# Newton stage of a two-layer transformer block: the third softmax kernel formed transposed, remainders in halves, a new order

## The reference, cut to what matters

```python
kernel1 = softmax(einsum('bhnd,bhmd->bhnm', Q, K_l))    # 256 x 64 per head
kernel2 = softmax(einsum('bhmd,bhkd->bhmk', Q_l, K_l))  # 64 x 64
kernel3 = softmax(einsum('bhmd,bhnd->bhmn', Q_l, K))    # 64 x 256
V0 = kernel2.T / max(sum(kernel2, axis=-2))
for _ in range(6):                                      # Newton iterations
    KV = K @ V
    V = 0.25 * V @ (13 I - KV @ (15 I - KV @ (7 I - KV)))
SV = (kernel1 @ V) @ (kernel3 @ values)
out = SV @ w_proj
```

## Time and profile before

| what | us |
|---|---|
| median of 3 runs (2047.25 to 2049.43) | 2047.33 |
| profiled execution, its own time | 2049.97 |
| its span, first to last instruction | 2048.2 |
| TensorE busy in the span | 1849.3 |
| VectorE busy | 1646.0 |
| ScalarE busy | 1097.7 |
| GpSimd busy | 932.4 |
| mean granted TensorE clock, share of full | 0.976 |

### The profile page before, as it was taken

The page is one execution under the profiler, slowest core; times in us unless marked ns, Lnnn a source line. Parts: engine busy times, 40 slices in busy tenths (PEclk is TensorE's granted clock), DMA queues, the critical chain, the costliest instruction groups (busy, mean ns, idle before and its releaser), DMA issues.

```text
span 2048.2 us, 66118 instructions
## 1 busy us (share of the span) xinstructions
PE 1849.3 (90%) x27529; PEld 1414.5 (69%) x27529; DVE 1646.0 (80%) x3968; ACT 1097.7 (54%) x2880; POOL 932.4 (46%) x913
## 2 busy tenths in 40 slices
PE   3999899998999688868999999999999999967887
PEld 2888566665788556656777777777777777754666
DVE  6666799999566699966888888888888888857997
ACT  1444233332344466645666666666666666636664
POOL 2000688886000277733444444444444444426886
PEclk9999999999899899988999999999999999998999
DMA  4000000000000000000000000000000000000001
GB/s 118 1 1 1 1 1 2 2 2 2 1 1 1 1 1 1 1 1 3 3 3 3 3 4 3 3 3 3 3 3 4 3 3 3 3 2 1 21 22 42
DMA packets 14601, 14.44 MB, mean 7 GB/s; under 512 B 1440, under 2 KB 12128, under 8 KB 14304
## 3 DMA queue, kind: packets, MB, share of 16 engines
q1 hardware_dynamic: 11104, 8.83, 1.5%
q10 hardware_dynamic: 3200, 1.37, 0.3%
HBM read 6.01 MB, written 4.19 MB: 5 GB/s over the span
## 4 chain that ended last, share of the span: by engine, by line
PE 62%; DVE 27%; issue 6%; ACT 4%; POOL 1%; DVEq 0%; DMA 0%; POOLq 0%; SPq 0%
PE acc L473 6%; PE acc L450 6%; PE acc L1666 6%; DVE arena L576 5%; PE acc L1656 5%; PE acc L1678 4%; DVE acc L894 2%; DVE arena L571 2%; DVE arena L907 2%; DVE arena L884 2%; PE acc L757 2%; PE acc L1708 2%; PE acc L464 2%; PE acc L1606 2%; PE acc L1589 2%
## 5 line engine op out<-in xcount | busy, mean ns | idle before, releaser
L1506 POOL TENSOR_TENSOR arena<-arena 128x288 f32<-128x288 f32 (+1 forms) x384 | 293.1, 770 | 456.6 <-ACT arena L1413 397.8
L931 POOL TENSOR_TENSOR arena<-arena 128x960 f32<-128x960 f32 (+2 forms) x74 | 177.7, 2401 | 299.5 <-DVE arena L900 204.6
L1413 ACT ACTIVATE arena<-acc 64x288 f32<-64x288 f32 x384 | 155.6, 405 | 141.0 <-PE acc L1684 133.7
L1232 DVE SCALAR_TENSOR_TENSOR arena<-acc,arena 128x288 f32<-128x288 f32 (+1 forms) x384 | 157.1, 409 | 68.6 <-PE acc L1678 38.9
L679 POOL TENSOR_TENSOR arena<-arena,quadcol 128x512 f32<-128x512 f32 x64 | 79.3, 1258 | 247.4 <-DVE arena L546 247.4
L425 ACT ACTIVATE arena<-acc,wib 128x256 f32<-128x256 f32 x256 | 100.5, 475 | 149.9 <-PE acc L464 149.9
L1017 PE MATMUL acc<-wguT,arena 128*128 128x352 f32 x256 | 105.2, 493 | 48.1 <-DVE arena L884 47.2
L1678 PE MATMUL acc<-arena 64*64 64x72 f32 (+1 forms) x3072 | 135.1, 224 | 11.7 <-DVE arena L1232 11.6
L1666 PE MATMUL acc<-arena 64*64 64x72 f32 (+1 forms) x3072 | 133.0, 223 | 13.5 <-DVE arena L1223 12.8
L1666 PEld LDWEIGHTS acc<-arena 64*64 64x64 f32 x3072 | 110.8, 133 | 46.5 <-issue 44.1
L1223 DVE SCALAR_TENSOR_TENSOR arena<-arena 128x256 f32<-128x256 f32 x192 | 107.7, 561 | 43.6 <-ACT arena L1413 41.0
(11 more groups left out here) (238 smaller groups left out, 4890.9 us busy)
## 6 DMA issues: line engine op xcount, KB each, us to landing
out_dram<-X SPq DMA_DIRECT2D x3, 1024.0 KB, 5.2
out_dram<-X SPq DMA_DIRECT2D x1, 512.0 KB, 3.2
wi<-in_wiT_dram ACTq DMA_DIRECT2D x1, 256.0 KB, 5.4
wout<-in_woT_dram ACTq DMA_DIRECT2D x1, 256.0 KB, 7.4
out_dram<-X SPq DMA_DIRECT2D x1, 256.0 KB, 2.3
out_dram<-X SPq DMA_DIRECT2D x2, 128.0 KB, 1.8
wqkv<-in_w_qkv_dram ACTq DMA_DIRECT2D x1, 192.0 KB, 8.3
arena<-in_w_down_dram SPq DMA_DIRECT2D x1, 176.0 KB, 3.0
```

The costliest lines, as they stand in the source:

```text
L931: pool.tensor_tensor(b3(y[k][:, part(u)]), b3(z[k][:, part(u)]), each(small[u % kept][:, 1, blocks(u)]), ALU.mult).then_inc(y_ready, 1)
L1232: dve.scalar_tensor_tensor(pm[s][:, group[g], cols], pn[s][:, group[g], cols], part, tm[s][:, group[g], cols], ALU.mult, ALU.add).then_inc ...
L1413: ins = act.mul(sq[s][rows, group[g], :], pn[s][other, group[g], 0:MW], part)
L1506: pool.tensor_tensor(tm[s][:, group[g], cols], pm[s][:, group[g], cols], sq[s][:, group[g], cols], ALU.subtract).then_inc(tm_ready, 1)
```

## The change

The third kernel is formed transposed at once. `scores3` and `max3` stay for the maxima (two reductions of two banks each in place of four), which are laid in rows of a mask, transposed (`turn_m3`) and added to spare rows of the queries (`lower3`); `keys` makes copies of the keys in which the other pair's rows hold ones. `turned3` then forms the lowered, transposed scores in one product, `exp3` exponentiates them in two instructions, and `start_w` gets the row sums from columns of ones in `vtok`. The 16 transposes and `copy3` go. The first kernel does the same with `expand_rows`, `masked_queries` and `lower1`, and the products with `pick` go. The second group's square and remainder are made in halves: ScalarE and VectorE each take 64 partitions of the product from PSUM and then change over. The queues are reordered. The second kernel's softmax works as before.

```diff
-            e3 = [cut(NP, SEQ) for _ in R]
+            kx = [cut(2, SEQ) for _ in R]
+            qm = [cut(2, SEQ) for _ in R]
+            kst = [cut(NQ, LM) for _ in R]
+            mov3 = [cut(2, P) for _ in R]
+            mov1 = [cut(2, SEQ) for _ in R]
-                def max3(n, s, q):
-                    dve.wait_ge(s3_done, n * NQ + q + 1)
-                    dve.tensor_reduce(sm[s][:, NMAX3, 2 * q:2 * q + 2], A[q].rearrange("p (t n) -> p t n", t=2), AX,
+                def max3(n, s, k):
+                    dve.wait_ge(s3_done, n * NQ + 2 * k + 2)
+                    dve.tensor_reduce(m3n[s].rearrange("p o (q t c) -> p (o q) t c", t=2, c=16)[:, 2 * k:2 * k + 2, :, 0],
+                                      psum[:, 2 * k:2 * k + 2, :].rearrange("p q (t n) -> p q t n", t=2), AX,
                                       ALU.max, negate=True).then_inc(max3_ready, 1)
+                def lower3(n, s):
+                    dve.wait_ge(m3T_done, n + 1)
+                    for t in range(2):
+                        ins = dve.scalar_tensor_tensor(mov3[s][:, t, :], mxp[0], pairmask[:, 1 - t:2 - t],
+                                                       qlx[s][:, 2 * t:2 * t + 2, :].rearrange("p h m -> p (h m)"),
+                                                       ALU.mult, ALU.add)
+                    ins.then_inc(mov3_ready, 1)
...
+                    for h, (rows, cols) in enumerate(halves):
+                        ins = dve.tensor_tensor(pairs(pm[s])[rows, :, :, LM:LM + HD],
+                                                kvp[s][rows, :, :, h * HD:(h + 1) * HD],
...
+                def remainder_half(n, s, it, h):
+                    rows, other = halves[h][0], halves[1 - h][0]
+                    iterate(dve, n, it, 1)
+                    dve.wait_ge(sq_done, step(n, it, 1))
+                    if h == 0:
+                        dve.wait_ge(sq_ready, turn(n, it, 1))
+                    dve.scalar_tensor_tensor(rm[s][rows, group[1], :], pm[s][rows, group[1], 0:LM], 7.0 * size[it],
+                                             pn[s][other, group[1], 0:LM], ALU.mult, ALU.subtract).then_inc(rm_ready, 1)
...
+                def lower1(n, s, t):
+                    dve.wait_ge(mxT_done, n + 1)
+                    dve.wait_ge(qm_ready, n + 1)
+                    dve.scalar_tensor_tensor(mov1[s][:, t, :], A[0][:, 0:SEQ], pairmask[:, 1 - t:2 - t], qm[s][:, t, :],
+                                             ALU.mult, ALU.add).then_inc(mov1_ready, 1)
...
+                def keys(n, s):
+                    act.wait_ge(qk_ready, n + 1)
+                    for t in range(2):
+                        ins = act.activation(kx[s][:, t, :], qkT[buf(n)][:, 1, :], ACT.Identity,
+                                             bias=rowhot[:, 2 - 2 * t:3 - 2 * t], scale=pairmask[:, t:t + 1])
+                    ins.then_inc(kx_ready, 1)
+                def masked_queries(n, s):
+                    act.wait_ge(qk_ready, n + 1)
+                    for t in range(2):
+                        ins = act.activation(qm[s][:, t, :], qkT[buf(n)][:, 0, :], ACT.Copy, scale=pairmask[:, t:t + 1])
+                    ins.then_inc(qm_ready, 1)
+                def exp3(n, s, k):
+                    act.wait_ge(s3T_done, n + 1)
+                    act.activation(flat(eT[s][:, 4 * k:4 * k + 4, :]),
+                                   psum[:, 2 * k:2 * k + 2, :].rearrange("p q n -> p (q n)"), ACT.Exp)\
+                       .then_inc(e3_ready, 1)
-                def copy3(n, s, q):
...
+                def square_half(n, s, it, h):
+                    rows, other = halves[h][0], halves[1 - h][0]
+                    act.wait_ge(sq_done, step(n, it, 1))
+                    if h == 1:
+                        act.wait_ge(rm_ready, turn(n, it, 1))
+                    act.mul(sq[s][rows, group[1], :], pn[s][other, group[1], 0:MW], 15.0 / (13.0 * size[it]))\
+                       .then_inc(sq_ready, 1)
...
+                    pool.tensor_tensor(kst[s], klx[buf(n)], rowhot[:, :].unsqueeze(2).broadcast_to([P, NQ, LM]), ALU.add)\
                         .then_inc(lk_ready, 1)
...
-                def turn3(n, s, q):
+                def turn_m3(n, s):
+                    pe.wait_ge(max3_ready, 2 * n + 2)
+                    pe.transpose(mxp[0], m3n[s][:, 0, :], ident[:, :]).then_inc(m3T_done, 1)
+                def turned3(n, s):
+                    pe.wait_ge(mov3_ready, n + 1)
+                    pe.wait_ge(kx_ready, n + 1)
                     for t in range(2):
                         for j in range(TPB):
+                            for q in range(NQ):
+                                mm = pe.matmul(A[q][:, t * SEQ + j * P:t * SEQ + (j + 1) * P],
+                                               kx[s][quad(q), t, j * P:(j + 1) * P], mov3[s][quad(q), t, :],
+                                               start=True, stop=True, skip_group_check=True)
+                    mm.then_inc(s3T_done, 1)
...
+                    for t in range(2):
+                        for j in range(TPB):
+                            for q in range(NQ):
+                                mm = pe.matmul(kvT[s][quad(q), t * P:(t + 1) * P], vtok[s][:, j, 2 * q + t, :],
+                                               eT[s][:, 2 * q + t, j * P:(j + 1) * P], start=(j == 0),
```

More of the change, by code:

```diff
@@ L1439, in a @@
                     if run:
-                        square(n, s, 0, 1)
+                        square_half(n, s, 0, 0)
                     if head:
@@ L1523, in g @@
                         remainder(n, s, 0, 0)
+                    if head:
+                        expand_rows(n + 1, o)
+                    if run:
                         remainder(n, s, 0, 1)
-                        remainder(n, s, 1, 0)
                     if head:
```

335 lines of the change are left out of this document (161 added, 174 removed), and 2 rows, old and new, of the table names.

## The result

The changed kernel takes 2080.51 us (median of four runs, 2078.34 to 2086.21) beside 2048.38 for the kernel before on the same chip: 1.0149 times as long, 95% interval 1.0132 to 1.0167, or 32 us. Forecast were 2041, in a range of 2000 to 2063.

A forecast was written before the change was run, and what follows sets the result against it. TensorE was taken to set the pace, VectorE to pass it after the change. 31 periods x (27.9 - 28.07) = -5.3, ramp +1.3, last block -2.4: -6.4 from 2049.97 gives 2043.6, set to 2041 for the median; range 2000 to 2063.

The forecast's parts named there:

- Putting it in order: Walk of the new order through one steady Newton block: VectorE's stretch plus the seam, 27.7 to 28.1 us, taken as 27.9.
- seam: Between blocks: about 4.0 us in which VectorE has only 2.4 us to do, so it idles 1.2 to 1.6.
- VectorE's stretch: From max2 to newton(4, 1) in a block: VectorE has work without a gap for 24.1 us.
- rival 3: VectorE's halves lose overlap on both sides: 0.7 us more per block, block 28.6, time 2063; chance 0.24.
- The latency that the halves save: Each Newton iteration's square and remainder: 0.85 us instead of 1.25, hidden in steady blocks, 2.4 gained in the last.
- The changeover, "nothing": ScalarE and VectorE swapping halves in each iteration: ScalarE's first half is done before VectorE's second, so no cost.
- TensorE's work: TensorE's busy time per block: 3.26 us removed and 1.31 added, so from 27.39 to 25.44.
- TensorE keeps the pace: First rival: VectorE's halves overlap like full-width work, TensorE sets the block at 26.9 us, time 2010; chance 0.26.
- Ends: Outside the steady blocks: kernel start costs nothing, the stage's ramp +1.3 us once, the last block -2.4.
- ScalarE's busy time: Per block: at least 6 us removed, new exponentials and copies added, so it falls to 16 or 16.5.
- 0.42 per half: Each VectorE half remainder, 256 elements per partition from PSUM: 0.417 us, 0.43 with the gap.
- VectorE's busy time: Per block, counted from start to start: 6.3 us removed, 9.8 added, from 22.9 to 26.4 to 26.5.

The follow-up runs named there:

- e1: Changed kernel with the second group's remainder whole again, from the copy in SBUF, ScalarE squaring both halves without waiting: 2059.18 us.
- e15: Changed kernel without the changeover, VectorE's two halves side by side where the whole remainder stands: 2140.26 us.
- e3: Kernel before with only the halves and the changeover between ScalarE and VectorE put in: 2142.98 us.
- e7: Kernel before with the halves but no changeover, ScalarE squaring both halves before VectorE takes its two: 2071.8 us.
- e17: Changed kernel with whole remainders, plus sixteen unread transposes per block given to TensorE: 2087.91 us.
- e19: Changed kernel as it is, plus sixteen unread transposes per block given to TensorE: 2098.22 us.
- e10: Changed kernel with the halves but no changeover, VectorE's first half one place earlier than the whole remainder stood: 2197.79 us.
- e2: Changed kernel with whole remainders, each issued twice, the first time into a spare tile: 2213.23 us.

## Why the prediction was wrong

The step that failed is **"Putting it in order", with the terms that it takes: a block of 27.9**. Its shape was right (VectorE without a gap from `max2` to `newton(4, 1)`, then a seam); the size of VectorE's stretch was not, nor was the way it took each iteration's halves to go.

- *VectorE's stretch: 24.1 us forecast.* In the timeline `max2` starts at 1400.79 and `newton(4, 1)` at 1425.40, and 0.37 later the next could start: 25.0. Of the 0.9 too little, 0.8 is the overlap lost in front of seven halves: each starts 0.03 after the end of a full-width instruction and not 0.08 before it (as at 1407.91). That was rival 3, which I had given 0.24. `lower3` takes 0.52 from start to start in place of 0.4, `lower1` 0.79 in place of 0.66, and the overlap kept at 1403.88 gives 0.1 back. The seam came out at the forecast's upper end: VectorE waits 0.49 + 0.42 + 0.72 = 1.6 there. Without these waits its queue fills 28.94 - 1.6 = 27.3 us, forecast 26.5, by rival 3 27.2. I had the rule and one side of it in a row, and counted only the side that the row showed. The sum closes, but it is a reading of the timeline: no run gives back the lost overlap alone, and work cut from VectorE returned 0.22 of itself.
- *"The latency that the halves save": 0.85 in place of 1.25 per iteration.* The way from ScalarE's first half to the last one's end takes 1.7 us per iteration in the changed kernel and 1.65 with whole remainders (e1): nothing is saved. VectorE's halves stand behind other work and come late.
- *The changeover, "nothing".* ScalarE waits 1.7 us per block for it. In the changed kernel it still saves 60 us against halves without it (e15); in the order before, it cost 71 (e3 against e7). My walk looked only at VectorE's waits for ScalarE, which are indeed absent, and not at the other direction.
- *TensorE's work: 25.44 forecast, 26.8 measured.* One of the four groups of transposes took a step of 0.44 in the blocks before and not 0.59. `turned3` fills 1.10 (from 1410.13, the end of the product before, to 1411.23) and not 0.90; `start_w` fills 1.01, as forecast. Work added or taken away moves the busy time by less than its own length: 2.20 put back in e17 and e19 add 1.76 and 1.80. That is 0.15 + 0.20 + 0.4; the last 0.6 or so I can't itemize.
- *"TensorE keeps the pace" as the other limit (26.9).* No run comes near it: with VectorE's load cut back to 23.2, by two means, the block stays at 28.2 to 28.3, with TensorE idle 1.6 us of it. By the table behind e15 the way from product to product through ScalarE and VectorE is what lengthens a block; that it also sets these 28.2 is argued and not shown. With whole remainders in this order the change would not have been faster either (e1, 2059), so the forecast's 0.26 for 2010 stood on a limit that isn't seen here.
- *Ends.* Forecast +1.3 for the ramp and -2.4 for the last block. The first product of the Newton iterations comes at 935.0 and not 932.1, and 0.7 of that lies before the stage: +2.3. Up to `start_w` the ramp is 1.1 longer, near the forecast; `start_w` itself took 1.98 for its 32 records, at the low clock, where I had left 1.11. The last block was to give 2.4 back, and the distance from its last `cross` product to the end of the stage is 2.1 longer instead. There the granted clock differs: it fell to 0.50 (1.2 GHz) in the changed kernel, and in the kernel before it was 1.00 (2.4 GHz) but for the last half microsecond. The first two rows are the changed kernel, the third is the kernel before:

```profile
1851.40:1861.60 10.20, 8.41 (x134) 6.56 (x134) 6.10 (x13) 2.26 (x7) 2.74 (x5) 0.50 0.01 3
1865.00:1871.60 6.60, 3.24 (x28) 1.58 (x16) 3.08 (x6) 0.00 (x0) 0.00 (x0) 0.50 0.00 1
1830.00:1837.40 7.40, 3.42 (x63) 2.14 (x60) 3.55 (x8) 1.55 (x2) 0.00 (x0) 0.97 0.00 0
```

  In the 10.2 us before the first of these TensorE was busy 7.05. At 0.50 `totals` (line 1797) takes 1.95, against 1.05 in the kernel before, and `project` 1.22 against 0.71; `turned1`'s two halves take 2.09, against 2 x 0.64 in a steady block. Together that is 2.2, as much as the last block came out longer.
- *Right:* ScalarE's busy time (16.7), 0.42 per half, a full-width instruction with a PSUM operand only behind a half's end, a large maximum in front of a full-width instruction at 1.13 to 1.14 from start to start. VectorE's busy time (26.3) meets the 26.4 to 26.5 of the sum by luck: that sum counted from start to start, and so counted it is 27.3.

What stays open: the 9 us that are left with whole remainders (no run has the third kernel's new form in the old order of the queues, or the new order with the old form), why the changeover saves 60 us in one order and costs 71 in the other, and which of the hops makes up the 28.2.

## What to carry to other kernels

Before trusting "engine X bounds this block", measure what 1 us of X is worth: add a known amount of work that nobody reads to X alone, and take a known amount from its rival. Divide by what the addition itself took. In the kernel before, a busy microsecond of TensorE, busy 97.6% of the block, was worth 0.77; in the changed one it is worth 0.37 at 92.5%, and one of VectorE 0.22 at 91%. A microsecond more on the way from one product to the next went with 0.8 more of block, and the same work of VectorE in two places (e10, e15) gave times 57 us apart: where the work stands counted for more than how much it is. No sum of busy times shows that. An instruction on half the partitions between full-width ones should be charged its full length and the overlap on both of its sides, until a row shows an exception.

## What the runs showed of the hardware that was not expected

- Two VectorE instructions lose their overlap in both directions between half and full width: 0.03 after the end at 1407.91, 0.02 after it at 1408.35, against 0.08 before the end for full width after full width. The Trainium skill, "VectorE: DVE Perf Modes", section "Two Vector instructions with no wait between them", says that one starting in another quadrant is held until all earlier ones have finished; by that rule the trace agrees also for the half at 1407.91. It agrees with the exception at 1403.88 too: that instruction touches SBUF alone, where the half before it had also started on partition 0 (only its PSUM operand started on partition 64), and it isn't held.
- ScalarE and VectorE, each reading another half of the partitions of one PSUM bank, kept their lengths where they overlapped by over 0.3 us (62 times from 1100 to 1750 us: 0.404 and 0.421 us, against 0.405 and 0.420 where they didn't overlap at all).
- A remainder with both operands in SBUF took 0.43 us when it started 0.04 us before a GpSimd operation on the same tile, and 1.02 when it started 0.30 us into it; there it ended 0.28 after that operation (e2, at 1400.96 and 1401.30).
